# Attention with two PSUM banks for the row maxima and three for the exponentials, where it was three and two

## What is computed

```python
q, k, v = proj(Wq), proj(Wk), proj(Wv)         # 16 heads of width 16
att = einsum('bhqd,bhkd->bhqk', q, k) * scale  # scale = 16 ** -0.5
att = where(causal, att, -inf)                 # T = 1024
att = softmax(att, axis=-1)
out = einsum('bhqk,bhkd->bhqd', att, v)
return einsum('btc,dc->btd', out, Wo)
```

## Time and profile before

| | |
|---|---|
| Median of three runs | 3301.03 us (3293.49 to 3303.26) |
| The profiled execution, its own time | 3296.3 us |
| Span of the profile, first to last instruction | 3294.2 us |
| Busy: TensorE / VectorE / ScalarE / GpSimd | 2624.9 / 1983.7 / 945.5 / 446.7 us |
| Mean granted TensorE clock, share of full speed | 0.892 |
| Waits of TensorE for the reduces of line 652 (profile part 5) | 45.1 us before matmuls |
| First attention | about 51 to 632 us of the span |
| Second attention | about 2055 to 2632 us |

### The profile page before, as it was taken

One profiled execution on the slowest core, in us unless ns is written; L12 is line 12 of the kernel. 1 busy time (PEld: TensorE's weight loads), 2 busy tenths in 40 slices (PEclk: granted clock), 3 DMA queues, 4 the chain that ended last, 5 costly groups with the idle time before them and its releaser, 6 DMA issues. The chain is left out here.

```text
span 3294.2 us, 38580 instructions
## 1 busy us (share of the span) xinstructions
PE 2624.9 (80%) x12216; PEld 1707.7 (52%) x12216; DVE 1983.7 (60%) x3875; ACT 945.5 (29%) x1701; POOL 446.7 (14%) x304
## 2 busy tenths in 40 slices
PE   6898988869999795666555545888889866999998
PEld 3454544458888553333223322444444435888887
DVE  4765657244453365999989994667556433545544
ACT  1344434322222233011211102244344412222222
POOL 0000000042330210211011110000000012112110
PEclk8898989989999897887778777799899977999999
DMA  2000000021110110000000000000000001001000
GB/s 106 17 9 22 9 18 1 7 103 39 43 46 0 39 57 7 7 7 7 13 0 13 0 0 7 29 17 22 10 10 9 1 8 65 33 32 64 32 32 25
DMA packets 19327, 79.41 MB, mean 24 GB/s; under 512 B 4696, under 2 KB 5720, under 8 KB 15192
## 3 DMA queue, kind: packets, MB, share of 16 engines
q1 hardware_dynamic: 19168, 77.36, 6.6%
HBM read 70.99 MB, written 2.16 MB: 22 GB/s over the span
## 5 line engine op out<-in xcount | busy, mean ns | idle before, releaser
L652 DVE CUSTOM_DVE_ANT_0 a_junk<-pair,a_mask 128x512 f32<-128x512 f32 (+3 forms) x768 | 394.1, 555 | 243.5 <-PE pair L496 228.6
L589 ACT ACTIVATE a_prob<-pair 128x512 f32<-128x512 f32 (+3 forms) x768 | 362.1, 490 | 422.6 <-PE pair L519 410.8
L519 PE MATMUL pair<-a_qx,a_kx 128*128 128x512 f32 (+3 forms) x768 | 332.5, 447 | 34.5 <-issue 20.6
L496 PE MATMUL pair<-a_kx,a_qx 128*128 128x512 f32 (+3 forms) x768 | 286.1, 426 | 52.3 <-DVE a_mx_raw L652 45.1
L474 PE MATMUL pair<-a_hc,a_w 128*128 128x512 f32 x512 | 260.4, 634 | 72.3 <-DMA a_w<-in_L_qkv 59.3
L519 PEld LDWEIGHTS pair<-a_qx,a_kx 128*128 128x128 f32 x768 | 147.3, 197 | 204.1 <-issue 127.8
L942 DVE TENSOR_TENSOR mx_h<-pair,mx_g 128x512 f32<-128x512 f32 x128 | 88.5, 692 | 268.1 <-PE pair L761 258.1
L496 PEld LDWEIGHTS pair<-a_kx,a_qx 128*128 128x128 f32 x768 | 153.4, 205 | 149.9 <-DVE a_mx_raw L652 121.7
L449 POOL TENSOR_SCALAR_AFFINE_SELECT a_prob<-a_prob 128x512 f32<-128x512 f32 x128 | 81.5, 637 | 1081.0 <-ACT a_prob L589 1081.0
L759 PE MATMUL pair<-mx_x_hi,mx_w_lo 128*128 128x512 f32 x512 | 201.5, 393 | 24.1 <-POOL mx_w_lo L823 21.5
L759 PE MATMUL pair<-m_x_hi,m_w_lo 128*128 128x512 f32 x448 | 178.4, 398 | 49.2 <-POOL m_w_lo L823 47.2
(11 more groups left out here) (246 smaller groups left out, 4919.7 us busy)
## 6 DMA issues: line engine op xcount, KB each, us to landing
m_raw<-in_L_cond_experts SPq DMA_DIRECT2D x18, 1024.0 KB, 4.8
mx_raw<-in_L_ffn_experts SPq DMA_DIRECT2D x24, 512.0 KB, 5.0
a_w<-in_L_qkv SPq DMA_DIRECT2D x16, 640.0 KB, 3.9
mx_wt<-expert_weights SPq DMA_DIRECT2D x8, 1024.0 KB, 4.6
a_hc<-h_stream SPq DMA_DIRECT2D x8, 512.0 KB, 3.3
r_w_ring<-in_r_q_w SPq DMA_DIRECT2D x8, 512.0 KB, 3.6
m_raw<-in_L_cond_experts SPq DMA_DIRECT2D x6, 512.0 KB, 3.4
x_stream<-in_x SPq DMA_DIRECT2D x1, 2048.0 KB, 10.3
```

The costliest lines, as they stand in the source:

```text
L496: nc.tensor.matmul(first_bank[t % FR][:, 0:c1 - c0], qx[:, next_buf, a, i * P:(i + 1) * P], kx[:, next_buf, a // 2, c0:c1], start=True, st ...
L519: nc.tensor.matmul(score_bank[t % SR][:, q0:TT], kx[:, buf, a // 2, j * P:(j + 1) * P], qx[:, buf, a, h * TT + q0:(h + 1) * TT], start=Tru ...
L589: nc.scalar.activation(prob[:, i % RING, a, q0:TT], score_bank[(i * GH + a) % SR][:, q0:TT], ACT.Exp, scale=SCALE).then_inc(s["b_exp"], 1)
L652: nc.vector.tensor_tensor_reduce(out=junk[:, t % 2, 0:cols], in0=first_bank[t % FR][:, 0:cols], in1=mask[:, m0:m0 + cols], scale=1.0, scal ...
```

## The change

One constant. `FR` was 3 and is 2, so `first_bank` has two of the five banks and `score_bank` has three; `SR`, `t % FR` and `t % SR`, and both waits follow.

```diff
@@ -223,7 +223,7 @@
 
 STEPS = [(h, j) for h in range(HALF) for j in range(4 * (h + 1))]
 NS = len(STEPS)
-FR = 3
+FR = 2
```

## The result

| | before | after |
|---|---|---|
| Median, us | 3300.18 | 3418.59 |
| Range, us | 3293.49 to 3303.26 | 3415.13 to 3426.75 |
| Ratio, 95% interval | | 1.0365 (1.0341 to 1.039) |
| Span of the profile, us | 3294.2 | 3417.3 |
| Mean granted TensorE clock | 0.892 | 0.874 |

The change makes the kernel slower by 118 us here and by 122 us in its second measurement (experiment 1), where +89 was forecast; the range held it, and the side was right. The table and the profile here leave out one disturbed execution of 3852.89 us (with it the median of the changed kernel is 3422.76 us), as the median of experiment 6 leaves out one of 6049.41 us; the profile is that of experiment 1. The text goes by its 122 us; the two profiles differ by 123.1.

What follows compares the result with a forecast made beforehand. The prediction took TensorE to bound a turn's first half and VectorE's reduces its second. Its terms, 76 + 14 - 13 - 10 + 22 = +89 us on 3296.3, gave 3385 us, range 3328 to 3452.

Steps and rivals of the forecast that it cites:

- What bounds: In a turn of attention: TensorE bounds the first half, VectorE's reduces the second, fed by TensorE through three banks.
- Term 1: Double turns: a pair of firsts costs a round trip, 1.47 us against 1.22; 5.4 us per turn, +76 us.
- Term 2: The two starts, firsts with projections alone at a mostly lower clock: about 7 us each, +14 us.
- Term 3: Third score bank gives back net 0.95 us per double turn (-13 us) and 5 us per closing turn (-10 us).
- Term 4: TensorE clock in double turns: seven long stretches at 1.2 GHz instead of four, 7.4 us each, +22 us.
- the clock rules: Rival, double turns: every turn gets a long stretch at the low clock, 3437 us; chance 0.24.
- no change: Rival, whole kernel: full credit of 84 us cancels 76 + 14, giving +6, 3302 us; chance 0.04.
- faster: Rival, first halves and closings: all 84 us of score waits return and losses halve, -39, 3257 us; chance 0.04.

Runs made afterwards that it cites:

- experiment 1: The changed kernel measured again without any edit, for an undisturbed profile: 3421.09 us, ratio 1.0364 to the kernel before.
- experiment 6: The kernel before with nine unread matmuls per double turn, two ahead of F37 and seven ahead of F40: 3299.86 us, ratio 1.0002.
- experiment 2: The changed kernel with two banks for the maxima, two for the exponentials and the fifth unused: 3438.80 us, ratio 1.0433 to the kernel before.
- experiment 10: The changed kernel with values 8 moved ahead of F39 and eight unread matmuls ahead of F39: 3387.35 us, ratio 1.0278 to the kernel before.
- experiment 5: The kernel before with all five banks for the exponentials' scores in the closing turn only: 3280.99 us, ratio 0.9963.
- experiment 7: The changed kernel with thirteen unread matmuls ahead of F39 in each double turn: 3368.03 us, ratio 1.0214 to the kernel before.
- experiment 11: The kernel before with its six steady turns written out instead of a loop: 3268.72 us, ratio 0.9924.
- experiment 9: The kernel before with five closing-turn score banks, nine unread matmuls behind the maxima and four at each turn's start: 3272.18 us, ratio 0.9921.
- experiments 4: The changed kernel with values 8 moved ahead of F39, no filler matmuls: 3410.74 us, ratio 1.0338 to the kernel before.
- experiment 12: The kernel before with five closing-turn score banks, both thin stretches filled with unread matmuls and the loop written out: 3237.69 us, ratio 0.9830.

## Why the prediction came out as it did

**What bounds, right.** The second half of a turn is VectorE's with TensorE feeding it through the ring of firsts. Experiment 2 shows it most plainly: the bank taken costs 140 us, the bank given returns 18.

**Term 1, right.** The 1.47 us per pair is there, the delays stand in the table, and with the clock kept up they are within 0.2 of the working at every step, 5.27 at F45 against 5.4. From F37 to F40 the delay grows by 1.32 us (4.49 - 3.17), where the working had 1.3; moving values 8 ahead (experiment 10) takes 0.8 of that away and no more, so the cover of values 8 is most of that step and not all of it.

**Term 2, right.** +7.7 in each start against 7. The granted clock there is 0.71, as in the forecast (0.74 before in the same window from F0 on), so the lone matmuls of 0.79 were the right ones to reckon with.

**Term 3, right for the closings, a little too large in the turns.** The closings gave 4.9 and 5.5 against 5 each (the 5.5 with the clock at 0.91 before and 0.95 after). In the first half F6's wait costs 0.6 (experiment 2), taken at 0.5, and the credit against it is 0.9, where S4_2, S2_2 and S1_1 had been put at 1.0 together. So a first half nets 0.3 (38.69 to 38.40) and not 0.5. The other 0.4 of the forecast, for S11_2 and S11_3, belongs to the second half; that half is 5.2 longer at full clock (31.75 against 26.57), where 5.4 - 0.4 = 5.0 was forecast. Together terms 1 and 3 are 0.4 a turn too small, 5 us in all. What it said of line 519's waits in the closing turn was wrong. They fell, but not to near zero:

```profile
PEld pair L519 <- ACT a_prob L589: 11.5, 19, 0.8
...
PE pair L519 <- ACT a_prob L589: 2.1, 8, 0.3
```

Before, the loads of that turn waited 16.5 and the matmuls 5.0. Three banks do not cover the exponentials' round trip either, and five nearly do: in experiment 5 the matmuls no longer wait, the loads still wait 6.7 us in ten waits, and the turn takes 27.57 against 29.69 and 34.59.

**Term 4, wrong twice.** This is the step that failed, and it carries 24 of the 33 us between forecast and result. The forecast was +22. The double turns give 114.5 (50.0 + 64.5) less 14 times 4.9 = 46, and experiment 7 gives nearly the same: 50 to 53 us back over a filled gap, less 6.4 us of shorter jumps.

The first mistake is the sentence "Between the second and third turn nothing differs but the clock". The end of the third turn also holds the jump of the loop, 3.35 us, which the earlier trace rows has in its 31.77. A window shows a length and a clock side by side and doesn't say that one made the other; busy 24.12 of 31.77 against 22.27 of 27.05 leaves 7.65 idle against 4.78, and that rise of 2.9 in idle time was there to be asked about. So of the price of 7.4 for a long stretch 3.35 was loop, and about 4 the clock (2.9 in experiment 11, where the jump no longer drew the stretch out).

The second is what was counted. The forecast charged only for long stretches, those in which the low level lasts into the next turn, four of fourteen before and seven after. That count was nearly right: by the windows a first half behind such a stretch had time at the low level four times before and eight times after (and the second attention's closing turn both times). But the falls inside the second halves, which came in thirteen of the fourteen turns before and in all fourteen after, were charged nothing, and they are what grew. The windows' lengths times the share of time at 1.2 GHz that their granted clocks imply (1.00 for full, 0.50 for low) give, for the double turns, 100 us at the low level before and 248 after: in first halves 35 and 55, in second halves 65 and 193. The low clock there now lies on the stretch where TensorE is the critical engine: values 8 costs 1.94 instead of 1.06, and S10_0 and F40 stand behind it. The forecast also looked only at the gap and the work behind it. The work ahead of the gap had become thinner too, by the round trips of term 1: TensorE was busy for 3.60 of the 4.97 us ahead of the stop, and the clock fell with the stop. Too high a price for a long stretch and none for the longer falls in all the turns partly cancelled: that the term came within 24 us is luck.

The rival "the clock rules" had every turn with a long stretch, and 3437. In the total it is 18 us too high and the forecast 34 too low; in the clock's own term the two missed by about as much, 74 and 22 against 46. Its mechanism did not come true either: the turn behind had low time in nine cases of fourteen. The Trainium skill, page "TensorE: Matmul & The Clock Gate", section "A second HAM failure mode: psum-queue depth-cycling", has the clock swing between its levels in a kernel that cycles through PSUM banks with small idle times of TensorE; by that rule all fourteen turns fall. The trace agrees, but the rule does not tell the two kernels apart: no double turn of the changed kernel in either attention has both halves at 1.00, and none of the kernel before has.

**The rivals of no change and faster, wrong.** The trace excludes them as argued: ScalarE's wait for scores rose from 410.8 to 534.4 although it had a bank more. The Trainium skill, same page, section "HAM oscillation — how this bites in real kernels" reports no further gain from more PSUM buffering in one matmul kernel; here a bank moved from one ring to the other costs 4.9 us in each turn of 65 at full clock, so for this ring the measurement decides otherwise.

**Open.** Why the jump is twice as long in the second attention (6.8 against 3.4), and is not in the kernels with 9 to 13 more matmuls in a turn, was not tried. Beside the jump at 308 in experiment 9 two packets on each of the two instruction queues were seen, but no run changed how instructions are fetched. How the count of falls depends on how much work stands behind a gap also stays open: experiments 4, 6 and 10 each moved it in a way that no rule used here had told.

## What to carry to other kernels

A ring of banks is deep enough when its depth times the consumer's pace covers the consumer's own time plus the round trip back (here 0.61 x 3 covers 0.70 + 0.77, and 0.61 x 2 doesn't), and this can be reckoned to 0.2 us from the trace before. Do not take a bank from the ring whose consumer is the bound of a stage: VectorE waited less than ScalarE before (228.6 us against 410.8), and its bank was the dear one. Give more banks to a stage in which the other ring is empty, by time and not once for the whole kernel. A price taken from two windows that "differ only in the clock" has to be tested on idle time too, and a thinner stretch on TensorE should be charged once for itself and once for the half-speed work behind it, if that work is on the path. When filler work is used to hold the clock up, look whether it moves anything else: here it also shortened the jumps of the loop by 6.5 us.

## What the hardware showed that was not expected

- Filling one idle stretch with matmuls that nobody reads moved the fall of the clock to the next thin stretch instead of removing it: 26.6 + 41.7 us in a turn instead of 27.1 + 38.7, ratio 1.0002. Filling both gained 16 us in the fourteen double turns of the kernel without the loop (910.2 against 926.2), though TensorE had more to do: 426.37 us busy in the seven double turns of experiment 12 against 423.80 before, in 19 us less.
- Falls came in or behind stretches with an idle time of 1.6 us on TensorE before and 2.8 us after, in four turns of the changed kernel within 0.1 us of its start, behind waits of 0.7 us; and, with those stretches filled, behind waits of 0.4 to 0.6 us round eight matmuls of 4 columns.
- The jump back of a register loop stopped TensorE for 3.3 to 6.8 us each time, 20.6 us over four jumps; at three of the four the clock fell while it stood, at one it was already low. The same loop with 9 to 13 more matmuls in each turn had jumps of 3.3 to 3.9 us only, 14 us over four. Writing the loop out gained 25 us (0.9924).
- A closing turn of one attention went from 34.6 us with two banks for the exponentials to 29.7 with three and 27.6 with five (experiment 5).
